# An attention stage with two heads side by side on 64 partitions each, in 64x128 row tiles, four row buffers and an unrolled step loop

## The reference

```
x = _layernorm(x + _L0_attn_ref(x, Wq, Wk, Wv, Wo))        # a0: rotary self-attention
x = _layernorm(x + _L0_xattn_ref(x, ctx_1024, ctx_1024))   # x0: cross-attention, causal, a slope per head
x = _layernorm(x + _L0_ffn_ref(...))                       # f0: 64 tokens of a batch: attention and MLP
x = _layernorm(x + _L1_attn_ref(...))                      # a1: attention with a Gaussian term
x = _layernorm(x + _L1_xattn_ref(ctx_1024, ctx_1024, x, mask, ...))  # x1: cross-attention with a mask
x = _layernorm(x + _L1_ffn_ref(...))                       # 8 experts, 2 of them for each token
```

```
scores = jnp.einsum('bhqd,bhkd->bhqk', q, k) / sqrt(8)     # + bias or mask
attn = jax.nn.softmax(scores, axis=-1)
out = jnp.einsum('bhqk,bhkd->bhqd', attn, v)
```

## Time and profile before

| what | value |
|---|---|
| median of three runs (lowest, highest) | 1138.33 us (1136.57, 1139.11) |
| span of the profiled execution | 1137.3 us |
| busy: PE, PEld, DVE, ACT, POOL | 866.6, 548.7, 652.5, 517.1, 155.7 us |
| mean granted TensorE clock | 0.859 of 2.4 GHz |
| a0: first maxima to last context | 69.4 to 206.1 us |
| x0 | 236.8 to 390.4 us |
| f0 | 453.0 to 493.5 us |
| a1 | 578.5 to 714.2 us |
| x1 | 743.5 to 931.3 us |

### The profile page before, as it was taken

The page is one execution under the profiler, slowest core; times in us unless marked ns, Lnnn a source line. Parts: engine busy times, 40 slices in busy tenths (PEclk is TensorE's granted clock), DMA queues, the critical chain, the costliest instruction groups (busy, mean ns, idle before and its releaser), DMA issues.

```text
span 1137.3 us, 21997 instructions
## 1 busy us (share of the span) xinstructions
PE 866.6 (76%) x7183; PEld 548.7 (48%) x7205; DVE 652.5 (57%) x1690; ACT 517.1 (45%) x867; POOL 155.7 (14%) x170
## 2 busy tenths in 40 slices
PE   6149998459999563856669998369999972899970
PEld 3015554325555332524425554235555552899970
DVE  5278884536666572535358884356656535455567
ACT  2216666515455531424416666414444541566640
POOL 5410000100000011000500000300000005502204
PEclk9659999659999886887659999779999985899995
DMA  4923332482223014100913330262212042212212
GB/s 164 245 75 58 57 57 90 139 125 45 54 46 98 1 41 91 34 1 29 194 37 63 63 62 1 73 104 44 44 34 37 15 165 93 77 46 63 68 40 72
DMA packets 109103, 80.82 MB, mean 71 GB/s; under 512 B 17344, under 2 KB 105280, under 8 KB 108112
## 3 DMA queue, kind: packets, MB, share of 16 engines
q1 hardware_dynamic: 105872, 69.73, 28.3%
q0 software_dynamic: 3168, 10.29, 2.6%
HBM read 49.61 MB, written 29.82 MB: 70 GB/s over the span
## 4 chain that ended last, share of the span: by engine, by line
PE 62%; DVE 11%; DMA 7%; SPq 6%; issue 5%; POOL 4%; ACT 4%; POOLq 0%; DVEq 0%; ACTq 0%
PE PS L447 11%; PE PS L423 10%; PE PS L405 9%; PE PS L1590 7%; PE PS L420 5%; PE PS L401 4%; PE PS L1600 3%; PE PS L459 3%; SPq L641 3%; DMA rows_q<-parts 3%; SPq L312 2%; DMA BIG<-MT 2%; PE PS L170 1%; POOL experts_x L1501 1%; DVE MS L581 1%
## 5 line engine op out<-in xcount | busy, mean ns | idle before, releaser
L581 DVE TENSOR_REDUCE MS<-PS 128x2 f32<-128x512 f32 (+1 forms) x544 | 340.5, 640 | 194.2 <-PE PS L423 190.8
L535 ACT ACTIVATE BIG<-PS 128x1024 f32<-128x1024 f32 (+2 forms) x288 | 260.3, 905 | 242.6 <-PE PS L405 241.1
L423 PE MATMUL PS<-BIG 96*128 96x256 bf16 (+1 forms) x1088 | 215.1, 283 | 49.4 <-DVE BIG L2136 36.1
L405 PE MATMUL PS<-BIG 128*128 128x256 bf16 (+1 forms) x1088 | 183.0, 268 | 6.9 <-DMA BIG<-MT 5.6
L447 PE MATMUL PS<-BIG,VA 128*32 128x256 f32 (+1 forms) x2176 | 163.4, 373 | 5.5 <-ACT OT L511 5.3
L423 PEld LDWEIGHTS PS<-BIG 96*128 96x128 bf16 x1088 | 99.9, 103 | 134.4 <-issue 65.9
L405 PEld LDWEIGHTS PS<-BIG 128*128 128x128 bf16 x1088 | 107.1, 99 | 40.2 <-issue 6.9
L1590 PE MATMUL PS<-OT,VA 128*128 128x128 f32 x736 | 96.6, 278 | 0.4 <-ACT OT L1647 0.4
L1590 PEld LDWEIGHTS PS<-OT,VA 128*128 128x128 f32 x736 | 91.3, 195 | 0.7 <-ACT OT L1647 0.7
L297 POOL TENSOR_TENSOR parts<-rbuf,parts 128x512 bf16<-128x512 f32 x34 | 40.1, 1186 | 263.0 <-ACT parts L222 262.7
L447 PEld LDWEIGHTS PS<-BIG,VA 128*32 128x32 f32 x2176 | 44.0, 108 | 60.5 <-issue 56.7
(11 more groups left out here) (220 smaller groups left out, 1058.6 us busy)
## 6 DMA issues: line engine op xcount, KB each, us to landing
BIG<-rows_q SPq DMA_DIRECT2D x64, 192.0 KB
rows_q<-parts SPq DMA_DIRECT2D x17, 384.0 KB, 3.3
rows_k<-parts SPq DMA_DIRECT2D x17, 384.0 KB, 2.7
BIG<-rows_k SPq DMA_DIRECT2D x64, 96.0 KB
BIG<-in_ex_w SPq DMA_DIRECT2D x3, 2048.0 KB, 11.8
rows_q<-parts SPq DMA_DIRECT2D x17, 256.0 KB, 3.3
BIG<-rows_k SPq DMA_DIRECT2D x64, 64.0 KB
OT<-experts_x SPq DMA_DIRECT2D x46, 64.0 KB, 1.8
```

What stands on the lines that cost most here:

```text
L405: last = nc.tensor.matmul(bank[:, self.offset[kt]:self.offset[kt] + n], g.K6[b.par][:, h, kt * P:(kt + 1) * P], g.Q6[b.par][:, h, lo:lo + ...
L423: last = nc.tensor.matmul(bank[:, a, :], g.Q6[b.par][0:MROW, h, qt * P:(qt + 1) * P], g.K6[b.par][0:MROW, h, 0:kw], start=self.bias is Non ...
L535: nc.scalar.activation(g.PT[grp % 2][:, 2 * (u % 2):2 * (u % 2) + 2, 0:self.width], g.bank2[u % 2][:, :, 0:self.width], ACT.Exp, scale=SCALE)\
L581: nc.vector.reduce_max(g.MS[:, qt, 2 * pair:2 * pair + 2], g.bank[4 + v % 2][:, 0:2 * kw].rearrange("p (a k) -> p a k", a=2), axis=AX_X).t ...
```

## The change

- Q6 and K6 hold a head on 64 partitions, two heads of a pair (`a` = 0, 1) on partitions 0 to 63 and 64 to 127. Each is now four buffers of half the size (`NBUF` = 4). The rows of the maxima are 62 and 63 of each half, ones come with the constants (`k_extra`, once, 8 DMAs).
- Scores of a head contract 64 rows, maxima 62, each as a matmul in one 64x128 row tile of the array. `phase` issues them by turns: a maxima matmul of head `a`, then a scores matmul of head 1-a. A bias comes last, for each head by itself, with all 128 rows.
- DVE reduces one head at a time over all its keys, 16 reductions per item in every stage (causal: three blocks of 128, then `join`). They are negated in the reduction.
- `parts_of_m` goes from DVE to POOL.
- Values of a group go in one visit (both key blocks), after odd pairs of heads; the turns of maxima stand after the pairs 1 and 5.
- SP loads item j+2 in step j, before the m rows of item j, with 12 DMAs (14 with constants or extra rows). `Split` writes three parts of the queries once (one DMA, 384 KB) instead of six (three DMAs, 768 KB).
- The step loop is unrolled for all engines, and the zeroing and the writing of ones are gone.

```diff
-MROW = 96
+MROW = 62
+NBUF = 4
...
-            if j["query"]:
-                for first, k in ((0, 3), (3, 2), (5, 1)):
-                    sp.dma_start(rows[:, first:first + k, :], s[:, 3 - k, :].unsqueeze(1).to_broadcast([P, k, CH]))\
-                      .then_inc(self.written[n % NPARTS].sem, 16)
-            else:
-                sp.dma_start(rows, s[:, :, :]).then_inc(self.written[n % NPARTS].sem, 16)
+            sp.dma_start(rows, s[:, :, :]).then_inc(self.written[n % NPARTS].sem, 16)
...
+        def maxima(b, u, a, qt, start):
+
+            rows = slice(64 * a, 64 * a + MROW)
+            first = P if self.causal and qt == 1 else qt * nqt * P
+            kw = P if self.causal and qt == 0 else nqt * P
+            return nc.tensor.matmul(g.bank[4 + a][:, first:first + kw], g.Q6[b.buf][rows, u, qt * P:(qt + 1) * P],
+                                    g.K6[b.buf][rows, u, 0:kw], start=start, stop=self.bias is None)
...
+        def phase(bm, be, u, a):
+
+            if bm:
+                after(pe, self.mx_done, H * bm.no + 2 * u + a - 1)
+            for i in range(nqt):
+                start = self.bias is None or i == 0
+                if bm:
+                    mx = maxima(bm, u, a, nqt - 1 - i, start)
+                if be:
+                    st = scores(be, u, 1 - a, i, start)
+            if bm and self.bias is not None:
+                mx = add_bias(bm, g.bank[4 + a], False)
+            if be and self.bias is not None:
+                st = add_bias(be, g.bank[2 * (u % 2) + 1 - a], True)
...
+        def step(j, bm, be, bc):
+            for u in range(8):
+                heads(bm, be, u)
+                if u == 1:
+                    if be:
+                        after(pe, self.mts_done, self.m_turned)
+                        turn_m(be, 1)
+                    if bc:
+                        values(bc, 3)
+                elif u % 2 == 1 and be:
+                    values(be, u // 2 - 1)
+                if bm and u == 5:
+                    after(pe, self.mts_done, self.m_turned)
+                    turn_m(bm, 0)
+                if bc and u % 4 == 3 and u // 4 < nqt:
+                    turn_context(bc, u // 4)
...
+            n, w = self.mx_blocks, P if self.causal else nqt * P
+            for a in range(2):
+                dve.wait_ge(*self.mx_ready.at(H * b.no + 2 * u + a + 1))
+                nc.vector.tensor_reduce(g.MS[:, 0:n, a, u], g.bank[4 + a][:, 0:n * w].rearrange("p (n k) -> p n k", n=n),
+                                        axis=AX_X, op=ALU.max, negate=True).then_inc(self.mx_done.sem, 1)
...
+            t.done(nc.gpsimd.tensor_copy(parts[:, :, :, 0, :], m))
+            nc.gpsimd.tensor_tensor(parts[:, :, :, 1, :], m, parts[:, :, :, 0, :], ALU.subtract)\
+              .then_inc(self.mb_ready.sem, 1)
...
+            for a in range(2):
+                heads = src.rearrange("r (u a) t -> r a u t", a=2)[:, a, :, b.no * w:(b.no + 1) * w]
+                for first, lo, k in {"q": [(0, 0, 3 * DH), (3 * DH, 0, 2 * DH), (5 * DH, 0, DH)],
+                                     "k": [(0, 0, 3 * DH), (3 * DH, DH, 2 * DH), (5 * DH, 2 * DH, DH)],
+                                     "x": [(XROW, 0, self.xrows)]}[n]:
...
+        def step(j, bm, be, bc):
+            if be:
+                m_rows(be, 1)
+            if j + 2 < self.nb:
+                self.load(sp, self.items[j + 2], rows)
+            if bm:
+                m_rows(bm, 0)
```

More of the change, by code:

```diff
@@ L133, in writes, with part @@
     def writes(self, n, i):
-        return sum(48 if j["query"] else 16 for m, j in enumerate(self.jobs[:n + 1]) if m % NPARTS == i)
+        return sum(16 for m in range(min(n + 1, len(self.jobs))) if m % NPARTS == i)
+    def part(self, n, i):
+        return self.g.parts[n % NPARTS][:, i if self.jobs[n]["query"] else 2 - i, :]
     def bank(self, job):
@@ L352, in __init__, with loads, steps @@
         self.cx_done = g.shared_sem("core_cx_done", nqt * nb)
[L353 to L375, removed]
+        self.chain = g.shared_sem("core_chain", nqt * nb)
+        self.m_chain = g.shared_sem("core_m_chain", 2 * nb)
+        self.joined = g.shared_sem("core_joined", 2 * nb if causal else 0)
+        self.feat = [g.shared_sem(f"core_feat{i}", 16 * sum(self.loads(n) for n in range(i, nb, NBUF))) for i in range(NBUF)]
+        self.m_in = [[g.shared_sem(f"core_m_in{i}{h}", 32 * nb // NBUF) for h in range(2)] for i in range(NBUF)]
+        self.items = []
+        for n in range(nb):
+            loads = sum(self.loads(i) for i in range(n % NBUF, n + 1, NBUF))
+            self.items.append(Item(self, n, 16 * loads))
+    def loads(self, no):
+        return 12 + (2 if self.xrows else 0) + (2 if self.extra is not None and no < NBUF else 0)
+    def steps(self, body):
+        for j in range(self.nb + 2):
+            body(j, *(self.items[j - lag] if 0 <= j - lag < self.nb else None for lag in range(3)))
     def bias_for(self, b, transposed):
@@ new lines, in scores, with add_bias @@
+        def scores(b, u, a, kt, start):
+            rows = slice(64 * a, 64 * a + 64)
+            lo, n = self.queries[kt]
+            return nc.tensor.matmul(g.bank[2 * (u % 2) + a][:, self.offset[kt]:self.offset[kt] + n],
+                                    g.K6[b.buf][rows, u, kt * P:(kt + 1) * P], g.Q6[b.buf][rows, u, lo:lo + n],
+                                    start=start, stop=self.bias is None)
+        def add_bias(b, bank, transposed):
+            bias = self.bias_for(b, transposed)[:, 0:P if self.causal else nqt * nqt * P]
+            if self.causal:
+                bias = bias.unsqueeze(1).to_broadcast([P, 2, P])
+            return nc.tensor.matmul(self.biased(bank), g.ident_bf[:, :], bias, start=False, stop=True)
@@ L500, in tensor @@
-        self.steps(pe, step, self.nb - 1)
+            self.turned += 1
+        self.m_turned = self.turned = 0
+        def step(j, bm, be, bc):
[10 more added lines that the diff above has]
+                if bm and u == 5:
+                    after(pe, self.mts_done, self.m_turned)
+                    turn_m(bm, 0)
+                if bc and u % 4 == 3 and u // 4 < nqt:
+                    turn_context(bc, u // 4)
+                if self.tail and u % 2 == 1:
+                    self.tail.run("tensor", pe, (j, u // 2))
@@ L502, in scalar @@
+        self.steps(step)
     def scalar(self, act):
@@ L541, in step @@
                     m_rows(bm, 0)
-                if self.tail and i is None:
+                if self.tail:
                     self.tail.run("scalar", act, (j, grp))
-        self.steps(act, step, self.nb - 1)
+        self.steps(step)
     def vector(self, dve):
```

368 lines of the change are left out of this document (144 added, 224 removed).

## The result

The changed kernel takes 1216.54 us (median of 4 runs, 1211.79 to 1217.78) against 1137.75 us before: a ratio of 1.067, with a 95% interval of 1.064 to 1.070. The forecast was 1135, its range 1103 to 1172. The loss is outside the range and on the side of rival 2, but larger than it.

The account below looks back on a forecast made before the run. PE was taken to bound a0, x0, a1 and x1, DVE close behind. Stage terms a0 0, x0 -12, f0 +13, a1 +2.5, x1 -6 total -2.5 on 1137.3; forecast 1135 us, eight in ten 1103 to 1172.

Parts of the forecast that it names:

- rival 2: m rows come late in every stage, held up by loads in flight; 1160 us at 1.5 us late; chance 0.17.
- 42 x 0.41 = 17.2: Start of f0: 42 loads ahead of the first m rows take SP 17.2 us, making those rows 5.5 us later.
- SP's load of 12 DMAs (4.9 us): Each step's load on SP, standing between the two halves' m rows, was taken to last 4.9 us.
- only 0.7 us to spare in a0: In a0, from the turn at pair 5, m rows could be 0.7 us late before the step grows.
- 10.6 for 8.4: A full step of f0 was to take 10.6 us instead of 8.4; three such steps, +7 us.
- in f0 it is busy 6.5 of 8.5 at 1.00: Argument against a falling PE clock: in f0 PE ran at 1.00 though busy only 6.5 of 8.5 us.
- Rival 4: PE's clock falls for good, as PE is busy two thirds of a0's step; over 1200 us; chance 0.03.
- rival 3: Row-tile pairs run one after the other, 1180 us, or overlap by half, 1152 at 0.14 per pair; chance 0.12.
- A change of tiling: PE switching between row tiles and full array was taken to cost 0.09 us, bounds 0 to 0.17.
- rival 1: Change of tiling is cheap (0 to 0.05 us), loads as quick as before; 1113 us, or 1092 at 0; chance 0.22.
- DVE starves four times a step: In a0 and a1 DVE idles about 0.75 us four times a step, 3.0 in all; step 14.9 for 14.2.
- DVE's work: DVE's busy time per step of a0 and a1: 16 reductions at 0.66 us plus two contexts, 12.0 us.

Follow-up runs that it names:

- neighbouring heads: Changed kernel with pairs formed of heads u and 8+u, so each load reads 8 heads adjacent in DRAM; ratio 0.978 to the kernel before.
- the version with both edits: Changed kernel with neighbouring heads, and SP's key loads moved behind the m rows, query loads staying ahead; ratio 0.975 to the kernel before, 0.973 when timed again.

## Why the prediction was wrong

**The step that failed** is the price of a load on SP: "Sixteen loads take from 447.00 to 453.57, 0.41 each on SP", carried over to "42 x 0.41 = 17.2" in f0 and to "SP's load of 12 DMAs (4.9 us)" in rival 2. The number was right for the row it came from and wrong for the new loads, whose source takes every second head: 0.58 to 0.82 each. I priced a DMA by its size and its row count and did not look at the pattern of its source, which stands in the diff. From it follow the late m rows: 12 loads take 9.4 us, instead of "only 0.7 us to spare in a0" the m rows are 1.6 to 3.7 us late there in all six steps that load, and in a1, with 14 loads, 3.1 to 4.0 in five of six. With this price put right, by neighbouring heads, the whole loss is gone and the end of x1 is 101 us earlier.

A second step failed beside it: f0 was priced at full clock ("10.6 for 8.4"), and against a lower clock stood only "in f0 it is busy 6.5 of 8.5 at 1.00", a row of the kernel before. A step of f0 is 12.3 us at 0.50 in the changed kernel and in the versions with neighbouring heads alike. So of f0's loss a part has nothing to do with the price of a load: with neighbouring heads the stage and the stretch ahead of it are still 21 us longer than before, where the forecast had +13.

The Trainium skill (Perfetto Trace Analysis, What "DMA-bound" means) counts the issuing engine's sequencer as a limit of its own and says that its window in the profile is the generation of descriptors, not data movement. The trace agrees in so far as SP issues for 9.4 us in a step whose DMA share is 0.17; that this time is the making of descriptors is the page's word, no run here shows it.

**Rival 2** had the place (m rows behind the load, from the turn at pair 5) and the mechanism half: late because of what stands ahead in SP's queue, not because transfers in flight hold them up. At 1160 it was too low by 57 us, as it took the delay as 1.5 us, left the starts of the stages as they were, and did not count on the clock falling behind the waits.

**Rival 4**, the clock, was given 0.03 and only as a whole. It came in part. In the changed kernel the clock falls to 0.5 four times in the middle of a0 (at 99, 116, 133 and 164 us, for 3.4 to 10.2 us; three times in its second profile) and five times in a1, each time within 2.5 us of the end of a wait of PE for m rows; with neighbouring heads it holds 1.00 from 81 us to the last 3 us of a0. In f0 it stands at 0.50 from 458 to 563 us while PE is busy 12.30 of 12.30 us, and also where of its m rows one pair alone is late, by 1.0 us (0.50 from 410 to 495 in the version with both edits). Of the 101 us that neighbouring heads give back, 16 lie ahead of the first maxima of the stages (67.0 to 61.3 us in a0, 31.1 to 29.6 in x0, 66.8 to 61.3 in f0, 32.3 to 29.1 in x1), where SP's queue is shorter. The other 85 lie within the stages; PE's waits behind m rows account for up to 62 of them, and what is left, some 23, is for the half clock and anything else, not split by a run.

**What held.** Two row tiles of a pair start within 0.01 us of each other in x1 (within 0.02 in a0), and pairs follow each other by 0.11 to 0.12 (rival 3 is out). A change of tiling costs 0.09 each way; in x1, from the version with both edits:

```profile
800.03 0.28 PE L410 MATMUL PS<-BIG 62*128 62x256 bf16 x1
800.03 0.28 PE L417 MATMUL PS<-BIG 64*128 64x256 bf16 x1
800.15 0.27 PE L410 MATMUL PS<-BIG 62*128 62x256 bf16 x1
800.15 0.27 PE L417 MATMUL PS<-BIG 64*128 64x256 bf16 x1
800.36 0.39 PE L426 MATMUL PS<-mask_q,ident_bf 128*128 128x512 bf16 x1
800.58 0.38 PE L426 MATMUL PS<-mask_k,ident_bf 128*128 128x512 bf16 x1
800.89 0.28 PE L410 MATMUL PS<-BIG 62*128 62x256 bf16 x1
```

From the second pair to the mask 0.21 = 0.12 + 0.09, from the second mask to the next pair 0.31 = 0.22 + 0.09. So rival 1 is out as well. Steps of x1 are 19.1 (forecast 19.1), of x0 14.6 without the late m rows (14.9). DVE starves four times a step as forecast: twice 0.62 to 0.65 us ahead of a reduction and twice 0.82 ahead of a context, 2.9 in all for 3.0. What was too dear is DVE's work: it is busy 11.1 us of a step, not 12.0, since four reductions take 2.54 us and so follow each other by 0.62, not 0.66. So a step of a0 without late m rows is 14.1 and not 14.9: over 14 steps some 11 us.

**With the issue at its old price** the change would have done about this: the version with neighbouring heads has the end of x1 at 907.9, 23.4 us ahead of the kernel before, near 1114 us in all (an estimate: 1137.75 less 23.4). That is within the range, but 21 us better than 1135, so the single number would have been off as well. By stage, each with the stretch ahead of it: a0 -13.7 (forecast 0), x0 -15.9 (-12), f0 +21.2 (+13), a1 -4.3 (+2.5) and x1 -10.6 (-6). f0 is the one stage that is worse in it, and the one where the forecast was too mild.

## What to carry to other kernels

When a layout changes, read the new source pattern of every DMA, not only its size: price its issue from a row of the same pattern, or measure it alone, which took a program of 100 us. On an in-order queue ask how long the longest block is between two short transfers that something waits for; cutting one block of twelve in two gave back 75 us without making anything cheaper. A wait of TensorE can cost more than its length, where the clock falls behind it as in a0 here. And when a stage's work changes, ask at which clock it will run: f0's did not keep the 1.00 of the kernel before.

## What the runs showed of the hardware

- The time of an issue on SP depends on the pattern of the source: loads of 8, 16, 24 and 48 rows with 8 pieces of 512 bytes each take 0.33, 0.42, 0.40 and 0.45 us with neighbouring pieces and 0.72, 0.63, 0.82 and 0.63 with every second one. With more rows it can be less. Why is not shown.
- TensorE's granted clock stood at 0.50 through f0 (458 to 563 us) with PE busy 12.30 of 12.30 us of a step. With 32 more matmuls of 256 columns in a step it rose to 1.00 within f0, at 432 us of that run; in the kernel before it was 1.00 with PE busy 6.50 of 8.50 us.
- Chips gave the same kernel 1138 and 1175.6 us, with the whole difference in the stretch behind x1 (some 205 and 242 us), where the slower one has gaps on PE that the other lacks. Ratios to the kernel before on the same chip held: 1.067 twice, and 0.975 and 0.973.
- In x1 at a granted clock of 1.00, two matmuls in the two 64x128 row tiles start within 0.01 us of each other, and pairs of 256 columns follow each other by 0.12 us; a change between row tiles and the full array costs 0.09 us each way.
